# Loading the first blocks of the gated sum from the ScalarE queue before the routing walk has ended

## Time and profile before

| | before |
|---|---|
| time, median of 3 runs | 4432.44 us (4432.07 to 4436.84) |
| profiled execution, its own time | 4432.26 us |
| its span | 4430.5 us |
| routing walk, first gather to the last add | 2987.4 to 4295.6 us |
| gate computation | 4295.9 to 4331.2 us |
| gated sum, to its last store's issue | 4331.2 to 4424.5 us |
| busy share PE / DVE / ACT / POOL | 74% / 82% / 54% / 62% |

### The profile page before, as it was taken

One profiled execution on the slowest core, in us unless ns is written; L12 is line 12 of the kernel. 1 busy time (PEld: TensorE's weight loads), 2 busy tenths in 40 slices (PEclk: granted clock), 3 DMA queues, 4 the chain that ended last, 5 costly groups with the idle time before them and its releaser, 6 DMA issues. The chain is left out here.

```text
span 4430.5 us, 103464 instructions
## 1 busy us (share of the span) xinstructions
PE 3266.7 (74%) x25228; PEld 2350.0 (53%) x25229; DVE 3621.0 (82%) x10151; ACT 2404.3 (54%) x5817; POOL 2724.9 (62%) x2719
## 2 busy tenths in 40 slices
PE   7886877877787877878787877347888888887620
PEld 3335666666666666666666666244555555555410
DVE  8888989989898988989898989876666676676457
ACT  4435666666566656666665666454555555555310
POOL 3226766667666766667676665117777777777750
PEclk9988999999999999999999999558999999999855
DMA  6537767667677766777676766521121121111147
GB/s 221 176 124 222 220 207 212 206 208 218 206 212 207 221 203 204 212 208 219 195 221 206 221 200 185 194 95 22 30 34 31 30 34 31 31 30 30 26 83 279
DMA packets 367713, 677.14 MB, mean 153 GB/s; under 512 B 70294, under 2 KB 240482, under 8 KB 367074
## 3 DMA queue, kind: packets, MB, share of 16 engines
q0 software_dynamic: 157888, 420.64, 35.7%
q1 hardware_dynamic: 97474, 128.43, 8.3%
q10 hardware_dynamic: 111712, 120.75, 8.1%
HBM read 582.00 MB, written 87.58 MB: 151 GB/s over the span
## 5 line engine op out<-in xcount | busy, mean ns | idle before, releaser
L736 POOL DMA_INDIRECT KV<-kv_d,src_i x1564 | 1609.1, 1029 | 798.6 <-issue 438.1
L1370 POOL DMA_INDIRECT re_src<-src_tab_d,rsrc x1024 | 985.0, 962 | 311.9 <-issue 245.2
L997 PE MATMUL agg_ps<-msg,oh 128*128 128x264 f32 x3512 | 872.2, 392 | 12.7 <-DVE msg L827 12.7
L997 PEld LDWEIGHTS agg_ps<-msg,oh 128*128 128x128 f32 x3512 | 639.3, 192 | 130.2 <-issue 34.1
L956 PE MATMUL Q<-q,ohT 128*128 128x256 bf16 x5328 | 672.7, 277 | 1.7 <-issue 0.5
L827 DVE TENSOR_TENSOR msg<-KV,msg 128x1024 f32<-128x1024 f32 x439 | 538.4, 1226 | 154.9 <-issue 107.8
L885 ACT ACTIVATE off<-dst_f,wbase 128x4 f32 x447 | 132.9, 297 | 854.7 <-issue 806.6
L893 ACT ACTIVATE square<-iota_b,off 128x128 bf16<-128x128 bf16 x1784 | 568.1, 389 | 0.3
L835 DVE TENSOR_TENSOR prod<-KV,Q 128x1024 f32<-128x1024 f32 x443 | 538.0, 1214 | 3.3 <-issue 1.3
L839 DVE TENSOR_REDUCE lg<-prod 128x32 f32<-128x1024 f32 x443 | 535.5, 1209 | 0.2
L956 PEld LDWEIGHTS Q<-q,ohT 128*128 128x128 bf16 x5328 | 496.3, 99 | 64.1 <-issue 2.2
(11 more groups left out here) (259 smaller groups left out, 5618.6 us busy)
## 6 DMA issues: line engine op xcount, KB each, us to landing
q<-q_d ACTq DMA_DIRECT2D x446, 192.0 KB
y_d<-ex_y ACTq DMA_DIRECT2D x56, 448.0 KB
rg_ye<-y_d SPq DMA_DIRECT2D x7, 3584.0 KB, 12.0
KV<-kv_d,src_i POOLq DMA_INDIRECT x1564
nu_xs<-xs_d SPq DMA_DIRECT2D x7, 2688.0 KB, 11.8
re_src<-src_tab_d,rsrc POOLq DMA_INDIRECT x1024
kv_d<-pr_kv SPq DMA_DIRECT2D x49, 256.0 KB, 2.2
xs_d<-pr_xs SPq DMA_DIRECT2D x49, 256.0 KB, 2.3
```

What stands on the lines that cost most here:

```text
L736: pool.indirect_dma_start(out=KV[:, t % (KVR * G), :], out_offset=None, in_=k.kv_d, in_offset=bass.IndirectOffsetOnAxis(ap=k.src_i[:, t:t ...
L997: m = pe.matmul(agg_ps[:, 0:HEADS * HW], oh32[ring(s, 2)][:, t, :], msg[ring(s, 2)][:, t, :, :].rearrange("p h e -> p (h e)"), start=(t == ...
L1370: pool.indirect_dma_start(out=gs[:, t % (RING * RG), :], out_offset=None, in_=k.src_tab_d, in_offset=bass.IndirectOffsetOnAxis(ap=k.rsrc[: ...
```

## The change

Five of the six first loads are moved. The outputs `ye` of blocks 0 and 1 and x2 (`o`) of blocks 0, 1 and 2 are now issued by ACT, in step 172 of the routing walk, behind `turn_copy(175)` and `exps(173)` and a wait for all stores to `y_d`. Only `ye` of block 2 is still loaded by SP in `route_gates`. As the gates' stage has not yet begun, the loads go into room that is dead by then: `ye` of block 0 and all three `o` into `k.acc` (where xT stood), `ye` of block 1 into the room of the expert weights, which are now parts of one tile `ex_w`. The loop that stores block i and loads block i + 3 is the same.

```diff
@@ act: route_experts
+                def first_blocks():
+
+                    for i, n in enumerate(stored):
+                        act.wait_ge(n, 16 * (NB * UPB // 2))
+                    for i in range(SLOTS):
+                        rows = slice(i * CN, (i + 1) * CN)
+                        if i < len(k.ye):
+                            act.dma_start(k.ye[i], k.y_d[rows, :, :].rearrange("(w p) e f -> p w e f", p=P)).then_inc(k.y_in[i], 16)
+                        act.dma_start(k.o[i], k.x2_d[rows, :].rearrange("(w p) f -> p w f", p=P)).then_inc(k.y_in[i], 16)
+
                 def body(s, u, third):
                     turn_copy(s + 3)
                     exps(s + 1)
+                    if u and third == 0 and isinstance(u.block, int) and (u.block, u.at) == (NB, 1):
+                        first_blocks()
@@ route_gates
-        ye = [sb(f"rg_ye{i}", [P, CW, NE, D], F32) for i in range(SLOTS)]
-        o = [sb(f"rg_o{i}", [P, CW, D], F32) for i in range(SLOTS)]
+        ye = k.ye + [sb("rg_ye2", [P, CW, NE, D], F32)]
+        o = k.o
@@ sp: route_gates
+                def outputs(i):
+                    rows = slice(i * CN, (i + 1) * CN)
+                    sp.dma_start(ye[i % SLOTS][:, :, :, :], k.y_d[rows, :, :].rearrange("(w p) e f -> p w e f", p=P)).then_inc(y_in[i % SLOTS], 16)
+
                 def load(i):
                     rows = slice(i * CN, (i + 1) * CN)
-                    sp.dma_start(ye[i % SLOTS][:, :, :, :], k.y_d[rows, :, :].rearrange("(w p) e f -> p w e f", p=P)).then_inc(y_in[i % SLOTS], 16)
+                    outputs(i)
                     sp.dma_start(o[i % SLOTS][:, :, :], k.x2_d[rows, :].rearrange("(w p) f -> p w f", p=P)).then_inc(y_in[i % SLOTS], 16)
-                for i in range(SLOTS):
-                    load(i)
+                outputs(2)
@@ graph_layers
+            ex_w = sb(route, "ex_w", [P, NE * 2 * FF + NE * FT * D], F32)
+            block = lambda t, at: t[:, at:at + CW * NE * D].rearrange("p (w e f) -> p w e f", e=NE, f=D)
+            flat_acc = k.acc[:, :, :].rearrange("p w f -> p (w f)")
+            k.ye = [block(flat_acc, 0), block(ex_w, 0)]
+            k.o = [flat_acc[:, at:at + CW * D].rearrange("p (w f) -> p w f", f=D)
+                   for at in (CW * NE * D + i * CW * D for i in range(SLOTS))]
```

More of the change, by code:

```diff
@@ L1627, in route_gates @@
         tri = sb("rg_tri", [P, NE, NE], F32)
-        ye = [sb(f"rg_ye{i}", [P, CW, NE, D], F32) for i in range(SLOTS)]
-        o = [sb(f"rg_o{i}", [P, CW, D], F32) for i in range(SLOTS)]
+        ye = k.ye + [sb("rg_ye2", [P, CW, NE, D], F32)]
+        o = k.o
         landed, dve, a_in, a_ok, added = (nc.alloc_semaphore(f"rg_{n}") for n in ("landed", "dve", "act_in", "act", "added"))
-        y_in, stored = ([nc.alloc_semaphore(f"rg_{n}{i}") for i in range(SLOTS)] for n in ("y_in", "stored"))
+        y_in = k.y_in
+        stored = [nc.alloc_semaphore(f"rg_stored{i}") for i in range(SLOTS)]
         with nc.Block() as block:
@@ L1794, in graph_layers @@
             k.sums = sb(route, "sums", [P, NW, RCOL], F32)
+            ex_w = sb(route, "ex_w", [P, NE * 2 * FF + NE * FT * D], F32)
[4 more added lines that the diff above has]
+                   for at in (CW * NE * D + i * CW * D for i in range(SLOTS))]
+            k.y_in = [nc.alloc_semaphore(f"rg_y_in{i}") for i in range(SLOTS)]
             k.weights = nc.alloc_semaphore("weights")
@@ L1797, in graph_layers @@
                 k.dtab = sb(ctx, "dtab", [P, NW, 6 * RH], BF16)
-                k.w1_sb = sb(ctx, "ex_w1", [P, NE, 2, FF], F32)
-                k.w2_sb = sb(ctx, "ex_w2", [P, NE, FT, D], F32)
+                k.w1_sb = ex_w[:, 0:NE * 2 * FF].rearrange("p (e c n) -> p e c n", c=2, n=FF)
+                k.w2_sb = ex_w[:, NE * 2 * FF:].rearrange("p (e f n) -> p e f n", f=FT, n=D)
                 k.b1_sb = sb(ctx, "ex_b1", [P, NE, FT], F32)
```

## The result

The changed kernel takes 4452.52 us (median of 7 runs, 4447.87 to 4455.6), the kernel before 4435.79 us (median of 7, 4432.07 to 4438.03). The ratio is 1.0037 with a 95% interval of 1.0025 to 1.0048, so +16.4 us with an interval of +11 to +21 us. The forecast was 4437.5 us, within 4431.5 to 4447: too low, and above the range. Slower by more than 0.2% had a chance of 0.23.

A forecast was written before the change was run, and what follows sets the result against it. The walk's end was taken as set by POOL's gathers, not ACT or DVE. Gain 0, held ACT 5.2 us with late gathers inside it, other terms 0: 4432.26 + 5.2 = 4437.5 us, range 4431.5 to 4447.

The forecast's parts named there:

- The moved loads: Gates' stage and gated sum: taking five loads off SP there was put at a gain of 0.
- three waits: DVE's waits for loads of blocks 4, 5 and 6 in the gated sum, 14.4 us, forecast to stay the same.
- (f): Other addresses of ye, o and the weights: same shapes, 0 us.
- SP's rows: SP's first loads in the kernel before: third to fifth issue 6.20, 3.38, 7.71 us; taken as ACT's upper bound, 18.45 us.
- the small stores' 0.32 us: ACT's 56 stores to y_d, 0.32 us each: lower bound of 1.6 us for ACT's five issues.
- T: Time ACT is free after its issues, forecast 4286.65 to 4289.9; first gathered operation due at T + 3.5.
- step (c): Loads issued on ACT drain slower beside gathers, at 0.77 until 4284; ACT free at 4289.9, costing 6.8 us.
- the 5.2 taken: Delay of the walk's end by held ACT, taken between 3.5 us (no slowing) and 6.8 us; own case, chance 0.50.
- step (d): Twelve gathers after 4268.2 at 1.6 us each beside the loads: 4.3 us late, inside the 5.2 of (c).
- Rival 2: POOL's last twelve gathers starve beside the loads once their pace passes about 1.7 us: 4446 to 4450 us, chance 0.20.
- one small store beside gathers: A 448 KB store leaves the gathers' 1.25 us pace as it is; used against rival 2, lower bound 0 for (d).
- The later of the two counts: (c) and (d) end at the same DVE operation, so the later counts, not the sum: inside 5.2 us.

The follow-up runs named there:

- e1: Changed kernel with all six loads back on SP in the gates' stage, only the new room left; ratio 1.0019 against the kernel before.
- e3: Changed kernel with four loads on ACT in step 172, the last o on SP; ratio 1.0007 against the kernel before.
- e4: Changed kernel with the same five loads on ACT, but behind its last Exp of the walk; ratio 1.0028 against the kernel before.
- f1: The changed kernel again, on a chip where all gathers have landed before step 172; ratio 1.0022 against the kernel before.
- h1: Changed kernel with PE's expert products cut and only the three o loads on ACT in step 172; 4431.0 us, one execution.
- g3: Changed kernel with PE's expert products cut and three loads on ACT; 4.1 us slower than g1, 58.7 us from store to add.
- h2: Changed kernel with PE's expert products cut and only ye of block 0 on ACT in step 172; 4431.9 us, one execution.
- g4: PE's expert products cut, four loads issued by POOL behind its last gather, the last o on SP; 14.9 us slower than g1.
- g1: The kernel before with PE's expert products cut, measure for the runs beside it; 4436.2 us, one execution.

## Why the prediction was wrong

**What held.** The moved loads are worth nothing: the stretch from the last add to the end is the same to 0.1 us, its three waits are the same (14.6 us), and the DMA engines had been idle before 4342.4. The room (f) costs nothing (e1). ACT is held, as SP's rows said and the small stores' 0.32 us did not, though from the fourth issue on and not from the third (0.59 us): e3, e4 and f1 show 9 us for the fourth and 17 us for both. With no gathers this gives nearly the time that the prediction had for it: 1.6 + 16.7 = 18.3 us, against 18.45. The rule of the Trainium skill, "DMA: Bandwidth & Descriptors", "Issuing engines are not separate DMA queues", that the time of issue is small, does not hold for these five loads. The path behind ACT is right too: free at T = 4305.5, the first gathered operation at 4308.97, T + 3.5.

**What failed, first: step (c), the drain beside gathers.** I gave the loads the 0.77 of the DMA engines that the gathers did not use, at full speed, and had ACT away for 21.7 us (T = 4289.9). It was 32.8 us. By its own working this step cost 6.8 us; the 5.2 taken is the middle between that and a drain with no slowing, for which no reason was given. DMA time cannot be shared out by the busy share seen when one user is alone. The two DMA queues over 16 us, before (4268 to 4284) and changed (4273 to 4289), as packets, MB and share of 16 engines:

```profile
q0 software_dynamic: 417, 0.13, 22.6%
```

```profile
q10 hardware_dynamic: 840, 3.44, 62.3%
q0 software_dynamic: 264, 0.09, 33.7%
```

A gather packet took 0.226 x 256 / 417 = 0.14 us of an engine alone, and 0.337 x 256 / 264 = 0.33 us beside loads (and 0.52 behind them, in h1; the trace does not part a packet's work from its waiting). The gathers took a larger share and got fewer packets through (16.5 instead of 26 for each us), and the loads got 215 GB/s instead of the 305 that I had reckoned with. With 32 packets to a gather (417 for 13), the pace is 1.9 us instead of 1.25.

**Second: step (d), the gathers' lateness.** I had 4.3 us from turns of one 4 KB piece for each row, 1.6 us for each gather. It was 10.4 us (g3). h1 and h2 show that the size of the piece is not what counts, so the picture behind the 1.6 us was wrong, not only its figure. Nor was its count of turns right: a gather is 32 packets, on average two for each DMA engine and not eight, and an estimate by two turns (2 x 0.165 + 0.29 = 0.62 us, under the pace of 1.25) would have no gather late at all. The step also priced POOL's pace alone, while 8.1 of the 10.4 us lie between the last issue and its landing. Rival 2 put the point of decision at a pace of 1.7 us, and at 1.9 us it was passed: of what happened, the greater part is this rival, which I had given 0.20 because of one small store beside gathers. That row could not bear it. The store is 448 KB with some 30 us to the next; the loads are 10.1 MB back to back. The rule of the Trainium skill, "DMA: Bandwidth & Descriptors", "Queues, rings and completion order", has turns packet by packet: the trace has each 4 KB piece as one packet (840 packets for 3.44 MB), so the loads' packets were not long, and the gathers starved all the same.

**Third: each makes the other longer.** "The later of the two counts" is right (ACT's 17.5 us of lateness cover the gathers' 10.4), but the gathers and the loads slow each other. By the measured values of f1, ACT would be free 16.7 + 1.6 us after 4272.67 with no gathers (4291.0), and it was free at 4305.5, 14.5 us later.

By size: the case taken was 5.2 us, the change is 17.3 to 17.5 us in the walk, 10.4 of it the gathers alone and 6.9 the held ACT beyond them. Why a gather packet takes more than twice its time beside loads, and nearly four times for some us behind them, is open; only the size of the pieces was tried, and it is not that.

## What to carry to other kernels

Before moving a transfer earlier, ask whether anyone waited for it: here nobody did, and a wait that did exist, for slots, went with one slot more (-11 us). Do not fill idle shares of the DMA engines beside small indirect gathers that set the pace: here 7 to 21 us of full-rate load made the walk 4 to 10 us longer, in part because POOL has no reserve and in part because the last gathers land late. A large load issued on an engine's queue behind two or three others holds that engine until part of them has gone through (9 us for the fourth, 17 us for the fourth and fifth, 31 beside gathers), and costs at the engine's next duty, be it an instruction or the meeting of the engines.

## What the runs showed of the hardware that was not expected

- POOL's loads of 896 rows showed as 1 us each, but its drain at the end of the stage lasted 35.5 us (g4; 13.1 in the kernel before), and DVE waited 20 us at the meeting for it. The drain ends 3.6 to 5.0 us after POOL's last gather has landed (before, changed, g1, h1, h2). ACT does not wait so: in e4 its drain is 0.16 us, and the next stage began 0.5 us after its last issue ended, with the DMA engines still full.
- With three loads (2688 pieces) in its queue ACT was not held (0.59 us for the third), while SP, with three small loads ahead, was held 6.20 us at its third large one.
- On two chips PE's granted clock averaged 0.80 instead of 0.93 and the whole program took 1.3 times as long; no run shows why. The change makes the walk 17.5 us longer on the one kind and 10.9 us on the other (f1), where all gathers have landed before the loads begin.
